# Attention block: softmax sums divided in turned rows, and x loaded by columns

## What is computed

```
h   = layernorm(x)
Q, K, V = h Wq^T, h Wk^T, h Wv^T                 # 16 heads of 16
A   = softmax(Q K^T / 4 with later keys masked) V
y   = x + A Wo^T
z   = layernorm(y)
out = y + z W^T + b + sum over the 2 best of 8 experts of gate * ((z A_e^T) B_e^T)
```

## Time and profile before

| | |
|---|---|
| median of 3 runs | 393.17 us |
| profiled execution | 393.18 us, span 391.4 us |
| mean granted TensorE clock | 0.975 of 2.4 GHz |
| TensorE busy | 354.2 us, 90% |
| ScalarE busy | 279.5 us, 71% |
| VectorE busy | 209.7 us, 54% |
| DMA | 23.31 MB, mean 60 GB/s |

### The profile page before, as it was taken

One profiled execution on the slowest core, in us unless ns is written; L12 is line 12 of the kernel. 1 busy time (PEld: TensorE's weight loads), 2 busy tenths in 40 slices (PEclk: granted clock), 3 DMA queues, 4 the chain that ended last, 5 costly groups with the idle time before them and its releaser, 6 DMA issues.

```text
span 391.4 us, 6977 instructions
## 1 busy us (share of the span) xinstructions
PE 354.2 (90%) x2558; PEld 138.0 (35%) x2558; DVE 209.7 (54%) x711; ACT 279.5 (71%) x317; POOL 47.8 (12%) x75
## 2 busy tenths in 40 slices
PE   8967978899998999999999999998999899799874
PEld 3545524354333444423323233232322323222542
DVE  4555558455755654555447464546346543600785
ACT  2544438677887877888788887888878688799311
POOL 5011000000011100011121111211112111100040
PEclk9997969999999999999999999999999999999997
DMA  6479444222450022271000000000000000000001
GB/s 202 139 224 315 116 131 141 55 55 54 124 148 13 2 54 75 62 214 44 13 2 13 3 13 16 3 13 2 13 16 0 16 0 15 13 2 3 0 3 55
DMA packets 29380, 23.31 MB, mean 60 GB/s; under 512 B 15392, under 2 KB 25888, under 8 KB 29344
## 3 DMA queue, kind: packets, MB, share of 16 engines
q1 hardware_dynamic: 29344, 22.84, 19.8%
HBM read 12.35 MB, written 10.49 MB: 58 GB/s over the span
## 4 chain that ended last, share of the span: by engine, by line
PE 63%; DVE 20%; ACT 7%; issue 6%; POOL 2%; DMA 1%; DVEq 0%; ACTq 0%
PE acc L713 23%; PE scores L696 12%; PE aux L596 7%; ACT probs L814 6%; PE aux L651 5%; PE aux L637 3%; DVE probs L1010 2%; PE aux L662 2%; PE aux L602 2%; PE aux L623 1%; DVE ffn L1055 1%; POOL exp_gap L1216 1%; PE aux L644 1%; DVE gates L1083 1%; DVE parts L954 1%
## 5 line engine op out<-in xcount | busy, mean ns | idle before, releaser
L814 ACT ACTIVATE probs<-scores 128x1024 f32<-128x1024 f32 x272 | 260.2, 1032 | 69.1 <-PE scores L696 59.1
L713 PE MATMUL acc<-probs,v_aug 128*32 128x512 f32 (+3 forms) x1280 | 145.4, 545 | 1.3 <-ACT probs L814 0.9
L696 PE MATMUL scores<-q_stack,k_stack 64*128 64x512 f16 (+3 forms) x640 | 86.5, 352 | 3.7 <-ACT probs L814 2.0
L696 PEld LDWEIGHTS scores<-q_stack,k_stack 64*128 64x128 f16 x640 | 21.1, 94 | 103.6 <-ACT probs L814 80.3
L1010 DVE TENSOR_TENSOR probs<-probs,mask_sb 128x512 f32<-128x512 f32 (+1 forms) x80 | 44.2, 577 | 22.5 <-ACT probs L814 22.0
L713 PEld LDWEIGHTS acc<-probs,v_aug 128*32 128x32 f32 x1280 | 30.8, 110 | 49.8 <-issue 29.7
L596 PE MATMUL aux<-xT,wqkv_sb 128*128 128x128 f32 x192 | 26.3, 294 | 1.0 <-DVE xT L941 1.0
L596 PEld LDWEIGHTS aux<-xT,wqkv_sb 128*128 128x128 f32 x192 | 24.0, 203 | 5.4 <-issue 3.1
L952 DVE CAST parts<-qk 128x512 f16<-128x512 f32 x12 | 5.1, 427 | 36.5 <-ACT qk L806 36.5
L1207 POOL TENSOR_TENSOR rstd<-ve,minus_half 128x1 f32<-128x1 f32 x12 | 7.3, 608 | 101.6 <-DVE ve L932 101.6
L1211 POOL TENSOR_TENSOR rstd<-ve,minus_half 128x1 f32<-128x1 f32 x12 | 6.6, 549 | 103.8 <-DVE ve L1040 103.8
(11 more groups left out here) (146 smaller groups left out, 323.0 us busy)
## 6 DMA issues: line engine op xcount, KB each, us to landing
q_stack<-q_dram SPq DMA_DIRECT2D x32, 128.0 KB, 2.8
k_stack<-k_dram SPq DMA_DIRECT2D x32, 128.0 KB, 2.8
qk_dram<-qk SPq DMA_DIRECT2D x12, 256.0 KB, 2.5
x_sb<-x SPq DMA_DIRECT2D x3, 512.0 KB, 6.4
q_dram<-parts SPq DMA_DIRECT2D x12, 128.0 KB, 2.0
k_dram<-parts SPq DMA_DIRECT2D x48, 32.0 KB, 1.9
out<-result SPq DMA_DIRECT2D x12, 128.0 KB, 1.7
qk_dram<-probs SPq DMA_DIRECT2D x4, 256.0 KB, 3.3
```

The lines of the kernel that those rows point to most:

```text
L696: m = pe.matmul(scores[u % BANKS][:, j, col:col + n], k_stack[row:row + STACK, kb // TPC, 2 * i + p, kb % TPC * P:(kb % TPC + 1) * P], q_s ...
L713: m = pe.matmul(acc[32 * hp:32 * hp + 32, lo:CHUNK], v_aug[:, kb, QUAD * i + hp, :], probs[:, u % PROBS, hp % 2, col:col + CHUNK - lo], st ...
L814: act.activation(probs[:, u % PROBS], scores[u % BANKS][:], ACT.Exp, scale=EXP_SCALE).then_inc(exp_done, 1)
```

## The change

- **Sums.** `turn_sums` and `turn_back` are gone for the first 12 tiles. When two quads of heads (half m of the heads) are in `sums`, SP writes them to `sums_dram` (`store_sums`, one DMA of 512 KB) and reads them back in an order where numerator and denominator of each element lie on the same partition and each head's features come as rows (`load_sums`, 4 DMAs of 128 KB). VectorE divides one tile of 128 tokens per step, from 7 steps behind the group that ended the half (`DIVIDE_LAG`): a reciprocal 128x128 and a product 128x128. The result is what `o` takes as it is. `sums` has one buffer instead of three.
- **x.** x also comes transposed from DRAM (`x_t`), 512 KB a chunk. Mean and rstd of the chunk's four tiles are put in 32x32 blocks, turned by VectorE (`turn_rows`), written by SP as four DMAs of 8 rows of 128 bytes, and read back to all 128 partitions (`load_rows`, 512 KB). VectorE then subtracts and multiplies, 128x512 each, for both halves (`normalise_x`). `turn_x` is gone.
- **Q and K.** `project_qk` makes one of the four 128-feature blocks for 512 tokens, instead of four blocks for 128 tokens: 4 pieces a chunk, as before. The stacks of half m are loaded when its K is written.
- **Pieces.** 92 instead of 127. In the first chunk they begin at step 3 instead of 0.
- **The last four tiles.** Their half 0 is divided in the loop. `residual` puts x (a product with the identity) and half 0's part of `o` into their PSUM banks in the last step. Then half 1 is turned, divided and turned back as before, with half the transposes and half of `o`, and ScalarE copies y out (`keep_y`) instead of VectorE's addition.

```diff
-PRE_PIECES = ("turn_x", "project_qk", "project_v")
-POST_PIECES = ("turn_sums", "turn_back", "o", "turn_y", "ffn", "turn_gated", "lora")
+FIRST_PIECE = 3
+MEASURE_FROM = {c: FIRST_STEP[c - 1] - 3 for c in range(2, NCHUNK)}
+NORMALISE_FROM = {c: MEASURE_FROM[c] + TPC + 6 for c in range(2, NCHUNK)}
+POST_PIECES = ("o", "turn_y", "ffn", "turn_gated", "lora")
...
+            def store_rows(c):
+                sp.wait_ge(rows_turned, c)
+                to = rows_dram[c].rearrange("n (t b p) -> b (n t) p", b=QUAD, p=32)
+                for b in range(QUAD):
+                    sp.dma_start(to[b], turned_rows[32 * b:32 * b + 2 * TPC, :]).then_inc(rows_out, 16)
+
+            def load_rows(c):
+                sp.wait_ge(rows_out, 64 * c)
+                if c > 1:
+                    sp.wait_ge(scores_ready, FIRST_UNIT[c - 1])
+                else:
+                    sp.wait_ge(squared, len(FIRST))
+                sp.dma_start(rows[c % 2], rows_dram[c].partition_broadcast(P)).then_inc(rows_in, 16)
...
+            def store_sums(c, m):
+                sp.wait_ge(acc_read, NQUAD * c + 2 * m + 2)
+                sp.dma_start(sums_dram[c, m], sums[:, 2 * m:2 * m + 2, :]).then_inc(sums_out[m], 16)
+
+            def load_sums(c, m):
+                sp.wait_ge(sums_out[m], 16 * (c + 1))
+                if c >= 2:
+                    sp.wait_ge(o_psum, TPC * (c - 1))
+                rows = sums_dram[c, m].rearrange("(h n d) q t -> n q d h t", h=QUAD, n=2)
+                for n in range(2):
+                    for q in range(2):
+                        sp.dma_start(attn[q * P // 2:(q + 1) * P // 2, c % 2, m, n], rows[n, q]).then_inc(sums_in[m], 16)
...
                 store_first_k(m)
+                if m == KH - 1:
+                    store_rows(1)
                 sp.wait_ge(first_q_out[m], 16)
                 load_queries(0, m)
                 sp.wait_ge(first_k_out[m], 16 * 2)
+                if m == KH - 1:
+                    load_rows(1)
                 load_keys(0, m)
...
+                    if slot == 0:
+                        for c, m in SUMS_AT.get(s - 3, ()):
+                            load_sums(c, m)
+                        for c, m in SUMS_AT.get(s - 1, ()):
+                            store_sums(c, m)
...
+            def residual(n, w):
+                pe.wait_ge(exp_done, tail_units[n % TPC] + 1)
+                pe.matmul(w.bank[:, 0:D], ident_sb[:], x_sb[:, n, :], start=True, stop=False)
+                pe.wait_ge(divided, divided_upto(NCHUNK - 1, 0, n % TPC))
+                pe.matmul(w.bank[:, 0:D], attn_of(n, 0), wo_sb[:, 0, :], start=False, stop=False)
...
                 piece(s, 0)
+                if s == STEPS - 1:
+                    for t in range(TPC):
+                        run_piece("residual", TILES - TPC + t)
                 for n in GROUPS_AT.get(s, ()):
                     values_of(n)
...
+            def normalise_x(c, k):
+                n = KH * (c - 1) + k + 1
+                dve.wait_ge(xT_in[c], 16)
+                dve.wait_ge(rows_in, 16 * c)
+                x_rows = xT[:, k, :]
+                dve.tensor_tensor(x_rows, x_rows, rows[c % 2][:, 0, :], ALU.subtract).then_inc(centred, 1)
+                dve.wait_ge(centred, n)
+                dve.tensor_tensor(x_rows, x_rows, rows[c % 2][:, 1, :], ALU.mult).then_inc(xT_ready, 1)
...
+            def divide(c, m, t):
+                n = divided_upto(c, m, t)
+                num, den = (attn[:, c % 2, m, n, t * P:(t + 1) * P] for n in range(2))
+                if t == 0:
+                    dve.wait_ge(sums_in[m], 64 * (c + 1))
+                dve.reciprocal(den, den).then_inc(inverse_ready, 1)
+                dve.wait_ge(inverse_ready, n)
+                dve.tensor_tensor(num, num, den, ALU.mult).then_inc(divided, 1)
```

455 lines of the change are left out of this document (270 added, 185 removed).

## The result

The changed kernel takes **405.32 us** (402.83 to 407.60, 4 runs) where the kernel before, beside it, takes 393.40 us (4 runs): a ratio of 1.030, 95% interval 1.021 to 1.039. The forecast was 384.9 us, the range 376 to 394, and slower had 9 chances in 100. The profiled execution is the longest of the four, 407.60 us, its span 405.7, so sums taken from its trace grow by 14.3 us where the medians grow by 11.9.

The account below looks back on a forecast made before the run. TensorE was taken to bound the kernel (busy 354.2 of 391.4 us, 63% of the chain). From 393.18 us, -8.4 - 2.2 - 4 + 4.5 + 1.8 = -8.3 gave 384.9 us, range 376 to 394.

Parts of the forecast that it names:

- A: Twelve tiles after attention: five pieces in five steps, two steps freed, at most 0.1 us waiting left; -8.4 us.
- D: VectorE's divisions and waits: 1.5 us for seven crowded steps, 3 us for waits for the sums; +4.5 us.
- Rival 3: Floors only: waiting after attention moves rather than goes, y's addition behind gates and masks; 389.7 us, chance 0.12.
- B: Q, K, V of tiles 8 to 15: 30.9 us a chunk instead of 32.0, two chunks; -2.2 us.
- C: First chunk: first project_qk near 33, turns of 4.6 us, step 10 near 61 instead of 65.23; -4 us.
- E: The end: residual products ahead of the last values +3.8, less work in the tail -2.0; +1.8 us.
- Rival 4: Slower: trips of the sums, 15.3 us, don't fit in seven steps of 12.7; 400 us, chance 0.08.

Follow-up runs that it names:

- e1: Changed kernel with VectorE copying gatedT out of the bank before normalising the other tile's y: 398.87 us, ratio 1.014 to the kernel before.
- e6: Changed kernel with the reciprocal of the sums over one column instead of 128, so the sums are not divided: 401.24 us, ratio 1.021.
- e14: Changed kernel with the divisions of the sums moved to other steps and nothing else: 402.97 us, ratio 1.022.
- e11: Changed kernel with e1, e2, e3, first-chunk pieces one a step, Q and K kept in held, stack loads later, VectorE's bank reads first: 388.02 us, 0.986.
- e15: e13 with the first chunk's pieces beginning at step 4 instead of 3 and x normalised a step earlier: 384.37 us, ratio 0.975.
- e2: Changed kernel with the residual of three of the last four tiles behind the last values instead of ahead: 406.88 us, ratio 1.032.
- e4: Changed kernel with eight unread products added in steps 0 to 3 to keep TensorE busy: 405.97 us, ratio 1.030.
- e12: e11 with the reciprocal over one column instead of 128, so the sums are not divided: 382.47 us, ratio 0.970.
- e13: e11 with the divisions of the sums moved to other steps: 389.04 us, ratio 0.986.
- e10: Kernel before the change with VectorE's reads of the bank put ahead of normalising and masks: 389.79 us, ratio 0.991.
- e3: Changed kernel with the first chunk's rows of mean and scale stored and loaded earlier: 403.64 us, ratio 1.025.
- e8: Changed kernel with e1, e2, e3, first-chunk pieces one a step, Q/K kept in held, later stack loads, GpSimd normalising third and fourth chunks' x: 396.50 us, 1.004.

## Why the prediction was wrong

The forecast's sum was -8.3 us; the profiled span grew by 14.3 (the medians by 11.9). By its own terms, of which A and D are measured over the same steps, so that D's part stands inside A's:

- **A, the tiles after attention: -8.4 forecast, about +6 measured. This is the step that failed.** The least of their pieces fell by 0.40 us a tile, 4.8 in all, as in "15.63 - 15.23 = 0.4". The waits in their steps were to fall and doubled, from 10.4 us to 21.3. The sentence that failed is "At most 0.1 of waiting is left". It looked only at what releases turn_gated, and there it held in eight of the twelve tiles: 1.91 us a step at most, against a median of 2.60 before. I never asked what releases `lora`, the next piece. The change puts the other tile's `o` ahead of it, VectorE's program then puts that tile's normalising ahead of the copy, and the wait came back: the median lora step is 0.81 us over its least, and TensorE waited 8.6 us for gatedT in all. e1 shows it: with that copy first the waits in these steps are 13.0 us instead of 21.3, and where nothing else is in the way a tile takes 11.62 + 3.62 = 15.24 us, the forecast 15.3. That is so three times out of seven; the other four times the five steps from one ffn to the next take 11.9 to 14.2 us in e1. So A would have come to about -2 without this wait, and still not to -8.4. D's divisions are in the 21.3 with 2 to 3 us (19.1 in e6, 18.2 in e14).
- **Rival 3** had the right idea, waiting that moves rather than goes, and the wrong place and size: y's addition behind masks cost 3.2 us at two places (the fourth of the waits above), the copy of gatedT behind the normalising 8.6.
- **B, Q, K and V of tiles 8 to 15: -2.2 forecast.** The least fell by 1.3, and the waits in these steps grew by as much, from 2.9 to 4.3. In size unimportant.
- **C, the first chunk: -4 forecast, +3.6 measured** (steps 0 to 9 take 46.7 instead of 43.1). The start of the first project_qk was right. The turns behind it were not: I gave each 4.6 us; they start at 32.78, 40.90, 46.35 and 51.26, so they took 8.1, 5.5 and 4.9. The first ran at the lower clock; and the later ones wait for VectorE's copy of v out of the one bank, which stands behind the split and the masks in its program (1.11 us ahead of the third, 0.58 ahead of the fourth). The four norms took 9.8 us in their two steps and not 5.6. So the result lies beyond the upper bound, +3 "if the clock is at the lower level through two of the turns", although the clock was low through one turn only, until 38.4: what was missing is the waiting for the one bank, in the turns and in the norms. By step 20, where the moved pieces are in again, e11 and e15 are 9.0 and 9.9 us ahead of the changed kernel (79.7 and 78.7 against 88.7), by one piece a step, earlier rows and the order together.
- **D, the divisions: 1.5 forecast, about 4 measured (e6; 4.0 of waits after step 10).** A division's own price was nearly right: the reciprocal takes 0.95 us (forecast 0.88), the product 0.32 (0.29). The number of steps in which it costs was not. The 3 us for VectorE's waits for the sums were wrong the other way: VectorE waited 14.3 us for them, 1.1 in chunk 1 and, against the forecast, 7.4 and 5.7 in chunk 3, but the steps around these waits (10 to 18, 80 to 89, 112 to 120) took 1.81 to 1.86 us each but for one of 2.32: in chunk 3 no mask and no read for TensorE stood behind them. The trip itself was shorter than the 9.8 us of the forecast where it can be seen alone: 7.4 us from the end of the copy of `acc` at 257.4 to the first division at 264.8.

```profile
L1152 DVE RECIPROCAL held<-held 128x128 f32<-128x128 f32 x28 | 26.4, 945 | 14.3 <-DMA held<-sums_dram 14.3
```

- The reciprocal's slope, (945 - 155) / 127 = 6.2 ns a column with e6's 155 ns for one, is six times a product's 1.0. The Trainium skill (VectorE: DVE Perf Modes, "First, the fixed hardware budget") gives the iterative division a repeat count of 8. Read as eight times a product's slope, as I had read it, that is not what is measured; 6.2 lies nearer to the slope of 5.6 that I took.
- **E, the end: +1.8 forecast, +3.4 measured.** The last values start at 377.87 behind the residuals, 2.4 us after the last mask ends at 375.46, and 3.1 us after the last exp's end at 374.74; before they started with it (the earlier trace rows has 363.70, the last exp ended at 363.75). That is 3.2 us where I had 3.8, and moving three of the four residuals gives 0.9 of it back (e2). Of the +3.4, 1.5 goes with the clock: in the runs without the stretch at the lower clock (e4, e6, e14) the end takes 29.5 us, with nothing changed in it, which is +1.9 and the forecast.
- **Rival 4** (trips that don't fit) had the sign and was not the cause: in the loop nothing on TensorE waited for a trip of the sums.

Open: what makes up the remaining 20 us of waits in steps 10 to 135. e12 says that the long reciprocals are worth 4 to 6 us there, e13 that moving them to other steps is worth nothing. Apart from e6 and e12, which don't divide the sums, no experiment took work off VectorE without giving it to GpSimd.

## What to carry to other kernels

When pieces are taken out of a schedule, list for each piece that remains what now stands ahead of its operand on the engine that makes it, not only what stands ahead of the piece. A removed piece that cost 0.1 to 0.3 us may have been the slot in which another engine did its waiting. And a product behind a long first wait of TensorE should be priced at the lower clock: in all fourteen kernels here in which the first project_qk had to wait (1.7 to 7.1 us) it took 3.5 to 3.75 us, and in e15, where values and scores fill the time up to it, 1.98. (A busy start is no warrant: in e10 the first project_qk didn't wait and took 3.28, the clock having fallen at 22.0.) Whether filling the wait or shortening it is worth more, these runs don't say: e3 and e15 have other edits or scatter of the same size.

## What the hardware showed unexpectedly

The normalising of y (fp32, 128x256, one operand in SBUF and two scalars) takes 0.81 us where it starts just behind GpSimd's addition to yb, and 0.40 in the one place where that had just ended. In e15 a normalising that starts later in the addition takes 0.59:

```profile
229.11 0.72 POOL L1375 TENSOR_TENSOR yb<-y,biases_sb 128x256 f32<-128x256 f32 x1
...
229.90 0.40 DVE L1186 TENSOR_SCALAR yln<-y,mv,rstd 128x256 f32<-128x256 f32 x1
```

```profile
131.46 0.73 POOL L1397 TENSOR_TENSOR yb<-y,biases_sb 128x256 f32<-128x256 f32 x1
...
131.75 0.59 DVE L1201 TENSOR_SCALAR yln<-y,mv,rstd 128x256 f32<-128x256 f32 x1
```

The loops of the 17 traces have 204 such normalisings. The 194 that start while GpSimd's addition runs take 0.59 to 0.82 us, and every one of them ends 0.15 us after the addition ends; the other 10 take 0.40. So it looks as if VectorE isn't slowed in them but waits for the addition to end. The long reciprocal, with one operand, keeps its 0.94 to 0.95 us in the three places where a pass of GpSimd runs at its start (e8).

So half of the 0.81 us that the normalising ahead of gatedT takes is not VectorE's work but a wait for GpSimd; e8 shows the same with a product of 0.29 us that took 1.08 and also ended 0.15 us after GpSimd's pass. The Trainium skill (SBUF — State Buffer, "SBUF: two separate sides") says that GpSimd and VectorE share a pair of ports which the one that starts first holds for its whole instruction, against a VectorE operation in a mode that uses two ports or with two operands in SBUF while GpSimd reads SBUF. For e8's product and masks, which have two operands in SBUF, the traces agree; that the normalising of y runs in a mode with two ports, no run here shows.

The times of one kernel go with the granted clock: the four runs of the changed kernel take 407.6 and 407.4 us at a mean granted clock of 0.955 and 0.948, and 403.3 and 402.8 at 0.961 and 0.965. In the end of the kernel alone, 3.4 us more at the lower clock go with 1.6 us more of time and with nothing else changed (e2 above). A difference of that size between two kernels says nothing before their clocks are compared.
